# A graph transformer with FFN, graph network and mixture of experts: outputs of two dense stages wait block by block or behind the next chunk's first units, the loop over attention heads written out, a low half taken in pieces

## The reference

```
x = x + graph_attention(layernorm(x), edges)   # 4 heads of 512; then a linear layer and a norm
x = x + ffn(layernorm(x))          # 4 experts: relu(x @ fc1_e) @ A_e @ B_e @ fc2_e, gated
x = x + graph_net(layernorm(x), mean of edge features)
                                   # h = relu([x, agg] @ W1 + b1); x + h @ W2 + b2
x = x + attention_and_moe(layernorm(x))        # 8 heads, 8 experts of 256, two norms
```

## Time and profile before

| | |
|---|---|
| median of 3 runs | 2376.66 us (2374.94 to 2377.1) |
| the profiled execution | 2372.45 us, its span 2370.4 us |
| PE busy (share of the span) | 2090.0 us (88%) |
| DVE busy | 1335.6 us (56%) |
| ACT busy | 719.0 us (30%) |
| POOL busy | 372.6 us (16%) |
| mean granted clock of TensorE | 0.949 |

### The profile page before, as it was taken

The page is one execution under the profiler, slowest core; times in us unless marked ns, Lnnn a source line. Parts: engine busy times, 40 slices in busy tenths (PEclk is TensorE's granted clock), DMA queues, the critical chain, the costliest instruction groups (busy, mean ns, idle before and its releaser), DMA issues. The chain is left out here.

```text
span 2370.4 us, 37213 instructions
## 1 busy us (share of the span) xinstructions
PE 2090.0 (88%) x13354; PEld 1822.1 (77%) x13355; DVE 1335.6 (56%) x3044; ACT 719.0 (30%) x1243; POOL 372.6 (16%) x308
## 2 busy tenths in 40 slices
PE   7976897899999999999998479998897999999576
PEld 5654575799989989998996358988785888888565
DVE  4444886343443444444443845455555788788667
ACT  3551101222221221222211112233243655555421
POOL 0000201000000000000000200111212545444444
PEclk9987898899999999999999789999998999999889
DMA  7651001212021211120001140021240112120442
GB/s 237 191 174 43 22 22 40 96 48 77 29 81 37 60 70 44 60 60 17 16 11 47 68 146 1 3 88 36 76 139 18 36 27 49 30 52 9 159 134 98
DMA packets 79016, 156.99 MB, mean 66 GB/s; under 512 B 7216, under 2 KB 22125, under 8 KB 77136
## 3 DMA queue, kind: packets, MB, share of 16 engines
q1 hardware_dynamic: 69340, 135.69, 19.0%
q0 software_dynamic: 4960, 11.49, 1.5%
q10 hardware_dynamic: 4616, 8.40, 1.0%
HBM read 104.19 MB, written 51.37 MB: 66 GB/s over the span
## 5 line engine op out<-in xcount | busy, mean ns | idle before, releaser
L130 PE MATMUL psum<-pt_hi,xn_hi 125*128 125x250 f32 x800 | 225.3, 282 | 1.6 <-DVE pt_lo L1068 1.6
L131 PE MATMUL psum<-pt_lo,xn_hi 125*128 125x250 f32 x800 | 223.8, 280 | 0.0
L132 PE MATMUL psum<-pt_hi,xn_lo 125*128 125x250 f32 x800 | 222.8, 278 | 0.0
L2137 POOL TENSOR_TENSOR mprob<-mprob,mrden 125x1250 f32<-125x1250 f32 x80 | 181.6, 2271 | 199.5 <-DVE mrden L2238 198.0
L130 PE MATMUL psum<-xt_hi,t_hi 128*125 128x512 f32 (+1 forms) x480 | 170.0, 354 | 2.8 <-DVE mx L1044 1.8
L131 PE MATMUL psum<-xt_lo,t_hi 128*125 128x512 f32 (+1 forms) x480 | 170.8, 356 | 0.0
L132 PE MATMUL psum<-xt_hi,t_lo 128*125 128x512 f32 (+1 forms) x480 | 170.3, 355 | 0.0
L970 ACT ACTIVATE prob<-prob,nb 125x1250 f32<-125x1250 f32 x40 | 53.6, 1341 | 350.4 <-DVE nb L1049 350.4
L1247 POOL TENSOR_TENSOR x_res<-x_res,beta 125x512 f32<-125x512 f32 x10 | 12.4, 1283 | 908.8 <-DMA x_res<-in_x 908.8
L2245 DVE TENSOR_REDUCE mmin<-psum 125x1 f32<-125x512 f32 (+1 forms) x240 | 127.0, 584 | 49.9 <-PE psum L2396 48.3
L130 PEld LDWEIGHTS psum<-pt_hi,xn_hi 125*128 125x128 f32 x800 | 151.2, 189 | 1.8 <-DVE pt_lo L1068 1.8
(11 more groups left out here) (497 smaller groups left out, 5811.1 us busy)
## 6 DMA issues: line engine op xcount, KB each, us to landing
slots_in<-slots_blank SPq DMA_DIRECT2D x12, 1282.5 KB, 11.1
cnt<-edge_counts SPq DMA_DIRECT2D x40, 305.2 KB
q_chunk<-q_store SPq DMA_DIRECT2D x40, 250.0 KB, 6.1
edge_attr<-in_attr SPq DMA_DIRECT2D x4, 1343.8 KB
slots_in<-slots_blank SPq DMA_DIRECT2D x3, 1539.0 KB, 18.4
moe_xg<-slots_in SPq DMA_DIRECT2D x17, 256.5 KB, 3.6
raw_WqT<-in_WqT SPq DMA_DIRECT2D x4, 1024.0 KB, 8.0
raw_WkT<-in_WkT SPq DMA_DIRECT2D x4, 1024.0 KB
```

Source lines behind the costliest of these rows:

```text
L130: nc.tensor.matmul(out, lh, rh, start=start, stop=False)
L131: nc.tensor.matmul(out, lh, rl, start=False, stop=False)
L132: return nc.tensor.matmul(out, ll, rh, start=False, stop=stop)
L2137: nc.gpsimd.tensor_tensor(prob[:, n % 4, :], prob[:, n % 4, :], rden[:, n % 4:n % 4 + 1].broadcast_to([P, N]), ALU.mult).then_inc(p_ready, 1)
```

## The change

It has five pieces.

1. `count_edges`: POOL's `xn_lo` is computed tile by tile, each piece behind the sums of its tile.
2. `pipeline` and SP's program: the loop over the first three heads is written out, on all engines. The inner loops over chunks stay.
3. FFN: the outputs of chunk c run on PE behind the first two hidden units of chunk c + 1 (`outputs`); the last chunk's stay at its end. DVE's additions move behind the second unit, the norm's steps by one or two units. DVE waits for the former outputs before it writes `lw` again.
4. FFN: `lora` waits for each block's low half before the block's products.
5. Graph network: the first output waits for each block's low half before the block's products.

```diff
@@ count_edges, POOL
-            nc.gpsimd.tensor_tensor(g.xn_lo[:], g.x[:], f32(g.xn_hi[:]), ALU.subtract)
...
                     nc.gpsimd.tensor_tensor(agg, agg, sums[:, par, 2 * EDGE_D:3 * EDGE_D], ALU.add).then_inc(sums_free, 1)
+                    tile = [a[:, bass.ds(2 * t2 + par, 1), :] for a in (g.xn_lo, g.x, g.xn_hi)]
+                    nc.gpsimd.tensor_tensor(tile[0], tile[1], f32(tile[2]), ALU.subtract)
@@ graph_attention, pipeline (the same in SP's program)
-        with eng.Fori(0, HEADS - 1) as h:
-            for tick, per in counts:
-                tick.enter(h, NC * per)
+        for h in range(HEADS - 1):
             with eng.Fori(1, NC - 1) as c:
...
-            for tick, per in counts:
-                tick.leave(HEADS - 1)
@@ dense_stages, DVE, between the low halves
                         if c and e == 0:
-                            if m < 2:
-                                moments(c - 1, m, x_added, 2 * (c - 1) + m + 1)
-                            if m == 2:
+                            if m == 1:
+                                for s in range(2):
+                                    add_out(2 * (c - 1) + s, s, out_done, x_added)
+                            if m >= 2:
+                                moments(c - 1, m - 2, x_added, 2 * (c - 1) + m - 1)
+                        if c and e == 1:
+                            if m == 0:
                                 seed()
-                            if m == 3:
+                            if m == 1:
                                 scales()
-                        if c and e == 1 and m < 2:
-                            first_normal(c - 1, m)
+                            if m >= 2:
+                                first_normal(c - 1, m - 2)
...
                 dve.wait_ge(lora_done, NE * c + NE)
+                if c:
+                    dve.wait_ge(out_done, 2 * c)
                 nc.vector.tensor_tensor(lw[:], core.bank(5)[:, 0:CH], wt[:, CH * c:CH * c + CH], ALU.mult).then_inc(lw_ready, 1)
-                for s in range(2):
-                    add_out(2 * c + s, s, out_done, x_added)
+            for s in range(2):
+                add_out(2 * LAST + s, s, out_done, x_added)
@@ dense_stages, PE
+            def outputs(c):
+                pe.wait_ge(lw_ready, c + 1)
+                for s in range(2):
+                    if c:
+                        pe.wait_ge(x_added, 2 * (c - 1) + s + 1)
+                    nc.tensor.matmul(core.bank(s)[0:P, :], lw[:, s * P:(s + 1) * P], f_sb[:], start=True,
+                                     stop=True).then_inc(out_done, 1)
+
             def hidden(c, e):
                 for m in range(KT):
+                    if c and e == 0 and m == 2:
+                        outputs(c - 1)
...
             def lora(c, e):
-                pe.wait_ge(u_free, UNITS * c + KT * (e + 1))
                 if e == 0 and c:
                     pe.wait_ge(lw_ready, c)
                 for k in range(KT):
+                    pe.wait_ge(u_free, UNITS * c + KT * e + k + 1)
...
-                pe.wait_ge(g_lo, MT * c + MT)
...
+                        if s == 0:
+                            pe.wait_ge(g_lo, MT * c + k + 1)
```

More of the change, by code:

```diff
@@ L922, in _ @@
             blank_slots(0, 3)
-            with sp.Fori(0, HEADS - 1) as h:
+            for h in range(HEADS - 1):
                 sp.wait_ge(raw_free, 2 * h + 2)
@@ L1897, in _ @@
                 lora(c, NE - 1)
-                pe.wait_ge(lw_ready, c + 1)
-                for s in range(2):
-                    if c:
-                        pe.wait_ge(x_added, 2 * (c - 1) + s + 1)
-                    nc.tensor.matmul(core.bank(s)[0:P, :], lw[:, s * P:(s + 1) * P], f_sb[:], start=True,
-                                     stop=True).then_inc(out_done, 1)
+            outputs(LAST)
             pe.wait_ge(e1_l, 2)
```

## The result

The changed kernel takes 2337.93 us (median of 4 runs, 2335.45 to 2339.17), the kernel before 2376.88 us beside it (4 runs; 2376.66 in the three runs shown ahead of the prediction). The ratio is 0.9837, 95% interval 0.9819 to 0.9854: 38.9 us, or 34.7 to 43.0 us, are gained. Forecast were 29.2 us, 2347.5 us, in a range from 2338 to 2357. The sign and the places are as forecast; the size was too small by a quarter of what was measured.

A forecast was written before the change was run, and what follows sets the result against it. PE was busy 2090.0 of 2370.4 us, so gains could come only from its idle 280 us or slow clock. Terms 15.8 + 4.9 + 6.0 + 2.5 = 29.2 us off 2376.66 gave 2347.5 us, range 2338 to 2357.

The forecast's parts named there:

- Part 1: Graph network's MLP: outputs waiting block by block remove waits in chunks 1 to 4 and slow clock; 15.8 us gained.
- Rival (c): Slow clock stretches don't depend on the waits and stay; 2350.8 us, chance 0.12.
- Part 2: FFN: outputs behind the next chunk's first two units, low-rank waits per block, norm steps moved; 4.9 us, bounds 2.5 and 6.5.
- Part 3: Attention's head loop written out: two jump stops go, a wait for DVE remains at each boundary; 6.0 us gained.
- the rule by itself: Head boundaries: a taken branch outside the prefetched pages stalls for fetching; stops would go whole, giving 9.9 us, not 6.0.
- (d): Head boundaries keep their 14.0 us, as ACT or DVE also fetch after a jump and are late; 2353.5 us, chance 0.07.
- (e): Written-out head code is met cold and each entry costs 4.94 us, making the kernel slower; 2392 us, chance 0.03.
- Part 4: Counting stage: low half in ten pieces, each costing DVE 1.05 us; 2.5 us gained, bounds 0.4 and 10.5.
- rival (b): Counting: each piece costs DVE all of its 1.28 us, so the part gives 0.4; 2349.6 us, chance 0.13.
- the rule on the shared ports: Counting: whichever of DVE and GpSimd starts first blocks the other throughout; each piece costs 1.28 us, the part gives 0.4.
- Is there slack?: Counting: DVE's and PE's steps are equally long; in the steady part DVE waited for free buffers only 1.66 us in all.
- Rival (a): DVE is not the limit while counting, PE's whole stop goes: 10.5 for 2.5 us; 2339.5 us, chance 0.10.

The follow-up runs named there:

- the undone wait: Changed kernel with one wait for all eight low halves ahead of the graph network's outputs, as before: 2354.01 us, ratio 0.9904 against the kernel before.
- the undone part: Changed kernel with POOL computing the counting stage's low half in one instruction again: 2347.59 us, ratio 0.9879 against the kernel before.
- The four undone parts: Changed kernel with one undone each: single low-half instruction 2347.59, PE's head loop 2343.39, FFN outputs and norm steps 2343.82, MLP's single wait 2354.01 us.

## Why the prediction was right, and where it fell short

**Part 1, the MLP: 15.8 forecast, 15.4 in the profiles, 16.2 by the undone wait.** Right nearly term by term: no hidden low half is waited for in any chunk, 3.9 us for W2 against "about 3.7", the slow stretch of chunk 0 now behind that wait, 3.6 us of clock against 3.3. Rival (c), the slow stretches stay, has fallen: they came back with the waits in the undone kernel. That POOL's additions are the cause, argued from the earlier trace rows, is shown by the kernel that cuts them short, but for 3.1 us.

**Part 2, the FFN: 4.9 forecast, 7.5 measured, over its upper bound of 6.5.** The boundaries gave 2.8 to 3.1 us (2.7 forecast) and the low-rank waits 1.3 (1.2). The step that failed is "PE's waits for hidden low halves between chunks cost 2.0 us in four stops", of which half was taken. The stops cost 3.7 us by the spacings, two of the six being in no list of waits, and nearly all of it went. The mechanism was right (the row scales no longer share a unit with the split of a weight), the term was mis-sized by a factor of three, because a stop was priced by its listed wait and a small restart, and only half of the list was taken.

**Part 3, the heads: 6.0 forecast, 5.6 by PE's loop put back, 8.7 between the two profiles.** The pattern is as forecast, three waits of 2.5 us and no issue stop. The 3.1 us more between the two profiles are the first two boundaries of the trace of before (1.7 us, of which 1.1 are its longer stops, 4.94 and 4.70 against 4.30 and 4.27) and the small steps of its first three heads (1.4 us), whose cause stays open. "As long the second" was read wrongly: the second stop is 4.70 us, so that the rule by itself would have given 9.6 us and not 9.9. The 6.0 itself is a difference of two rows of one trace, and holds. Rivals (d) and (e) have fallen: the boundaries don't keep their 14 us, and no issue stop shows in the code written out.

**Part 4, the low half: 2.5 forecast, 4.9 in the profiles, 5.4 by the undone part.** A piece costs DVE 1.00 to 1.04 us (1.05 forecast; the one-hots take 1.25 to 1.29 us, not 1.6), not its whole 1.28, since the one-hot's own 0.25 us pass within the piece. So rival (b) has fallen, and with it the rule on the shared ports taken to the letter. The step that failed is "Is there slack? [...] 1.66 us in all": DVE had 15.4 us of it, 12.4 at the changes of tile, where the rows of the steady part don't show it. By the starts of the zero products, tile 0 is 10.2 us shorter (25.8 to 15.6) and the nine others together 5.3 us longer (131.7 to 136.9): of nine pieces' 9 us PE lost some 5. Rival (a), that DVE is no limit, is half true: the whole stop of 9.10 us went, and some slow clock with it, but the 10.5 us of that rival didn't stay. Five short stops came, not nine (1.7 us by the list of waits), and PE's stops at the zero products, which the list calls issue, grew from 7.3 to 9.5 us; why these grew stays open.

The terms as the runs leave them are 15.4 to 16.2, 7.5, 5.6 to 8.7 and 4.9 to 5.4: 33 to 38 us, against 38.9 (34.7 to 43.0) measured. The four undone parts, low-rank waits aside, add up to 40 us by their ratios, but with an uncertainty of nearly 20, as that of the changed kernel enters four times. The two terms that were missed (FFN and low half) were missed downward, for two reasons: short stops of PE were valued at half of what the profile lists as waiting, and DVE's slack was read from the steady part alone. They account for some 5 us of the 9.7 by which the total was short, and the heads for up to 2.7 more by the two profiles. The rest is within what unchanged code and the medians vary by; how much of the total is luck can't be told.

## What to carry to other kernels

Price a stop of PE by the distance between the starts of its products, ahead of it, at it and behind it, not by the listed wait; short stops appear in no list, and the restart and a slow stretch of the clock come on top. To learn whether an engine has slack, total its waits over the whole stage before looking at single rows. In this kernel a low half or an addition on POOL held DVE up for nearly as long as it lasted (1.00 to 1.04 of 1.26 us). It is best put where DVE waits anyway, or onto DVE itself: there the same piece took 0.68 us, and tiles 1 to 9 together took 0.8 us more than before. Once a stop is removed, look for what is late next: two stops of 4.3 us gave 5.6.

## What was not expected of the hardware

**Unchanged code varies by as much as a term of the sum.** The stretch from the first T product to the first product on probabilities takes 42.8 to 45.8 us in the fourteen profiles. (Three of them, those with the value matrix's split moved, have no wait for it at the stretch's end; they lie at 43.2 to 44.3.) It goes with the granted clock. The changed kernel, and the kernel with the low half in one instruction (windows over the first 5 us of the stretch, and over the 16th to 25th):

```profile
409.42:414.42 5.00, 5.00 (x29) 0.66 0.76 262
424.42:434.42 10.00, 8.26 (x49) 1.00 0.00 1
```

```profile
415.21:420.21 5.00, 5.00 (x24) 0.52 0.78 268
430.21:440.21 10.00, 8.26 (x36) 0.83 0.00 1
```

PE stood for 16 us ahead of the first window in both and came back at 1.2 GHz. In all fourteen it is one of the two: where the first window stands at 0.66 or more (six profiles) the later one is full, where it stands at 0.58 or less (eight) a second slow stretch comes, PE being about as busy. What sets which of the two happens stays open: no run was made for it. The end of the kernel, behind the MLP, varies as well, from 659.3 to 663.3 us; what that goes with stays open. The trace of before has the shortest of the fourteen.

**POOL's first instruction of the counting stage comes 7 to 8 us late.** In the changed kernel ACT has the first sums by 257.04, and POOL adds them from 264.49 on:

```profile
256.71 0.33 ACT L714 ACTIVATE attr_sums<-psum 125x194 f32<-125x194 f32 x1 [15.67 <-PE psum L702]
...
264.49 0.80 POOL L664 TENSOR_TENSOR edge_mean<-attr_sums 125x64 f32 x1 [104.43 <-issue]
```

For the second tile it takes 0.2 us. The first delay is 7.0 to 8.0 us in all twelve kernels whose POOL begins the stage with these sums; POOL had last worked some 100 us earlier. Before, its first instruction of the stage was the long low half, 2.7 us behind ACT's high half. The cause stays open. PE isn't held up by it directly; it moves the first piece into tile 1.
